# Three loads ahead of the second layer's turns: requested by sync instead of scalar, and scalar's table load two values earlier

## The reference, cut to what matters

```python
def _L1_xattn_ref(queries, keys, values, Wq, Wk, Wv, Wo):     # 16 heads of 16
    q, k, v = split_heads(queries @ Wq.T), split_heads(keys @ Wk.T), split_heads(values @ Wv.T)
    attn = softmax(einsum('bhqd,bhkd->bhqk', q, k) * scale)
    return einsum('bhqk,bhkd->bhqd', attn, v) (heads joined) @ Wo.T
x = x + _L1_xattn_ref(_layernorm(x), ctx, ctx, ...)
x = x + (_layernorm(x) @ W.T + b + _layernorm(x) @ V_r @ C.T)
```

## Time and profile before

| | us |
|---|---|
| median of 3 runs | 754.68 (752.0 to 754.7) |
| profiled execution, time | 749.47 |
| profiled execution, span | 747.7 |
| PE busy | 727.4 (97%) |
| DVE busy | 462.2 (62%) |
| ACT busy | 311.0 (42%) |
| POOL busy | 271.7 (36%) |

### The profile page before, as it was taken

How to read it: one execution, slowest core, us unless ns; L and a number is a source line. 1 busy time by engine, 2 the same in 40 slices (tenths; PEclk the granted TensorE clock), 3 DMA queues, 4 the chain that set the end, 5 groups by cost and what they waited for, 6 DMA issues and landing times.

```text
span 747.7 us, 15572 instructions
## 1 busy us (share of the span) xinstructions
PE 727.4 (97%) x5802; PEld 560.2 (75%) x5802; DVE 462.2 (62%) x1052; ACT 311.0 (42%) x556; POOL 271.7 (36%) x320
## 2 busy tenths in 40 slices
PE   8999999999999999999999999999998999999996
PEld 6776667666766575699999998989766667677774
DVE  4678663557355668534444655738677868788625
ACT  1323211422142121245555554644246755565571
POOL 5976225423410624402201515124734435205051
PEclk9999999999999999999999999999999999999998
DMA  9898944631521595722453423454887776755001
GB/s 263 224 301 265 203 117 154 187 122 41 180 71 52 188 374 171 250 59 82 118 143 88 126 76 95 121 143 133 244 223 193 183 184 175 199 140 127 28 3 50
DMA packets 73069, 113.87 MB, mean 152 GB/s; under 512 B 14930, under 2 KB 59347, under 8 KB 71075
## 3 DMA queue, kind: packets, MB, share of 16 engines
q1 hardware_dynamic: 60928, 80.17, 37.4%
q10 hardware_dynamic: 5906, 17.03, 8.4%
q0 software_dynamic: 6160, 15.67, 6.7%
HBM read 84.27 MB, written 28.41 MB: 151 GB/s over the span
## 4 chain that ended last, share of the span: by engine, by line
PE 87%; DVE 4%; POOL 2%; ACT 2%; issue 1%; DMA 1%; another core or an unknown queue 1%; ACTq 0%; SPq 0%; DVEq 0%; POOLq 0%
PE ps L1463 15%; PE ps L1092 12%; PE ps L1472 7%; PE ps L1109 7%; PE ps L2186 5%; PE ps L2215 5%; PE ps L1128 5%; PE ps L2206 4%; PE ps L1140 3%; PE ps L1062 3%; PE ps L1034 3%; PE ps L2179 2%; PE ps L2160 2%; DVE mxh L1836 2%; PE ps L1069 2%; PE ps L2115 2%
## 5 line engine op out<-in xcount | busy, mean ns | idle before, releaser
L1836 DVE TENSOR_REDUCE mxh<-ps 112x2 f32<-112x750 f32 x128 | 115.1, 932 | 34.2 <-PE ps L2186 31.3
L1463 PE MATMUL ps<-rowsT,w 128*128 128x128 f32 x1120 | 130.8, 275 | 0.0
L1463 PEld LDWEIGHTS ps<-rowsT,w 128*128 128x128 f32 x1120 | 128.0, 192 | 0.1
L2036 ACT ACTIVATE d_pT<-ps 125x448 f32<-125x448 f32 x192 | 92.0, 549 | 46.3 <-PE ps L2206 42.0
L1092 PE MATMUL ps<-x1T,sw 128*128 128x448 f32 x256 | 101.3, 540 | 0.0
L1417 ACT ACTIVATE w<-rw 128x1024 f32 x70 | 73.8, 1056 | 64.4 <-PE ps L1463 57.3
L1092 PEld LDWEIGHTS ps<-x1T,sw 128*128 128x128 f32 x256 | 47.6, 190 | 38.8 <-issue 35.9
L1356 POOL DMA_DIRECT2D yscr<-y x35 | 19.7, 563 | 153.8 <-DVE y L1390 153.8
L1472 PE MATMUL ps<-rw,h 128*128 x280 | 66.4, 380 | 0.0
L2186 PE MATMUL ps<-kst,qst 96*112 96x375 bf16 x256 | 58.4, 332 | 3.0 <-DVE mxh L1836 1.6
L902 ACT ACTIVATE silu<-ps,sb 128x448 f32<-128x448 f32 x32 | 20.3, 634 | 96.9 <-PE ps L1092 88.9
(11 more groups left out here) (259 smaller groups left out, 1193.3 us busy)
## 6 DMA issues: line engine op xcount, KB each, us to landing
kst<-kscr SPq DMA_DIRECT2D x39, 378.0 KB, 5.3
rw<-in_rw SPq DMA_DIRECT2D x24, 512.0 KB
kscr<-ka SPq DMA_DIRECT2D x16, 567.0 KB
cT<-in_ctx_t SPq DMA_DIRECT2D x17, 378.0 KB, 4.7
ctxT<-in_ctx_t SPq DMA_DIRECT2D x16, 378.0 KB
ctxn<-in_ctx SPq DMA_DIRECT2D x16, 336.0 KB
qst<-qscr ACTq DMA_DIRECT2D x12, 448.0 KB, 7.0
rows<-xg SPq DMA_DIRECT2D x35, 128.0 KB
```

What stands on the lines that cost most here:

```text
L1463: last = mm(bank[1 + 2 * q + k][:, block], w12[:, k, c, block], rowsT[:, q, c * P:(c + 1) * P], start=c == 0, stop=c == C - 1)
L1836: V.tensor_reduce(mxh[:, b % 2, 2 * g:2 * g + 2], ps[0:S, p:p + 2, 0:K], axis=AX_X, op=ALU.max).then_inc(s["s_max"], 1)
L2036: A(pT[:, q % 2, k, :], bank[4 + k][0:KC, 0:QUAD * S], ACT.Exp).then_inc(s["p_ready"], 1)
```

## The change

SP issues the keys of 2, the queries of group 1 and the keys of 3, each behind one of the three context loads of batches 13, 14 and 15; ACT no longer issues them. The one-element Exp, and with it the table load, moves from between values 14 and 15 to between values 13 and 14. No data, buffer, wait of TensorE or amount of work is changed.

```diff
@@ -1671,6 +1671,12 @@
         for b in range(NV, NV + 3):
             sp.wait_ge(s["v_ps"], b + 1)
             load_context(sp, b + 3)
+            if b == NV:
+                load_keys(sp, 2)
+            elif b == NV + 1:
+                load_queries(sp, 1)
+            else:
+                load_keys(sp, 3)
         maxima(0)
         load_values(1)
 
@@ -2045,17 +2051,14 @@
         for c in range(C):
             chunk_out(a, "q", EARLY - 1, c, bank[7 - 2 * c])
         late_values(NV)
-        load_keys(a, 2)
         for m in range(C):
             query_out(a, EARLY - 1, m, bank[7 - 2 * m])
         late_values(NV + 1)
         late_values(NV + 2)
-        load_queries(a, 1)
         late_values(NV + 3)
+
+        A(outT[0:1, 0, 0:1], mhalf[0:1, 0:1], ACT.Exp)
         late_values(NV + 4)
-        load_keys(a, 3)
-
-        A(outT[0:1, 0, 0:1], mhalf[0:1, 0:1], ACT.Exp)
         late_values(NV + 5)
         store_queries(a, EARLY - 1)
         for b in range(B - 1):
```

## The result

The median went from 752.95 us (16 runs, 751.09 to 754.7) to 756.26 us (16 runs, 753.46 to 759.38). The ratio is 1.0049 with a 95% interval of 1.0037 to 1.0061, which is +2.8 to +4.6 us. The profiled execution takes 755.69 us (span 753.9).

What follows compares the result with a forecast made beforehand. TensorE was taken to bound the kernel, with 87% of the chain. ScalarE 0, table load 0 and maxima rows behind the keys (context 15 included) +0.8 us, on 754.7, gave 755.5 us; range 751.5 to 758.3.

Steps and rivals of the forecast that it cites:

- ScalarE and the table load, 0: ScalarE's program: nine issues removed gain 0 to 0.1 us, taken as 0; table load ahead of values 14 costs 0.
- SP's issue times: SP: queries issued from 538.5, keys of 3 from 541.8, maxima from 543.7 instead of 542.42; that alone costs nothing.
- Step 1: Queue q1: queries, 1.36 MB at 0.242 MB/us, take 5.6 us, done at 546.6.
- step 2: Queue q1: context 15 takes 2.1 us, done at 548.7, needed at 548.50; TensorE late by 0.2 us.
- rival C: TensorE's wait ahead of values 15: context 15 late behind the queries; +3 us, both ends bad +4.5; chance 0.20.
- Steps 3 and 4: Queue q1: keys of 3 done at 553.45, then maxima rows at about 554.0; TensorE, wanting them at 552.09, held 1.9 us.
- The upper end of my price for the stand: First transposed scores: at 0.227 MB/us the maxima rows land at 555.3, TensorE held 3.2 us, cost 2.1 us.
- The deduction for VectorE, 1.1 us: First transposed scores: VectorE is the chain there, so a 1.9 us hold costs 0.8 us, one of 3.2 us costs 2.1.
- A: First transposed scores: maxima rows stand behind the keys of 3 in SP's queue; +0.3 to +2 us; chance 0.42.
- B: SP's queue: the order harms nobody, all lands by 552.3; ±0, 754.7; chance 0.30.
- D: ScalarE: its issues were in the way, so faster by 0.1 us or up to 1 us, 754; chance 0.05.
- I price no clock: TensorE from 552 to 554: busy 1.45 of 2 us, granted clock stays at 1.00, so no clock cost.

Runs made afterwards that it cites:

- the maxima ahead: Changed kernel with the queries of group 1 and keys of 3 requested by sync behind the maxima of batch 0 and values of 1; 1.0010 against before.
- one query copy ahead: Changed kernel with only the first of three query copies ahead of context 15, two behind it ahead of the keys of 3; 1.0050 against before.

## Why the prediction was right, and where its steps were wrong

The forecast was +0.8 us, to 755.5, with a range to 758.3; the change cost +3.7 us [+2.8, +4.6] and came to 756.26. That the time is so close is luck: the cost is more than four times the forecast one, and the kernel before has a median over 16 runs (752.95) that lies 1.7 us under the one over 3 runs that I started from, which makes up for part of it. The place and the kind of the cost were foreseen; the two delays in the queue were sized too small.

- **What bounds the kernel: right.** TensorE is the chain in the stretch. Filling 2.6 us of it in the kernel before costs 1.0037, +2.8 us.
- **ScalarE and the table load, 0: right.** Stretch cost 0.0 and 0.9998 for the table load alone. (One reading was off: other copies of values follow ScalarE idle times of 2.0 to 3.0 us too, not only 2.36 and 0.51.) Taking nine issues off ScalarE gains nothing: with the maxima ahead it is 1.0010.
- **SP's issue times: right** to 0.1 us, and the wait of SP for its own issues cost nothing.
- **Step 1, queries (done at 546.6), and step 2, context 15 (done at 548.7, 0.2 us late): wrong, and this is the first step that failed.** The working divided bytes by a mean rate. The mean was right: packets by queue, after, from 542 to 549.9 us,

```profile
q1 hardware_dynamic: 411, 1.82, 98.4%
```

  so 1.82 MB, more than queries and context together (1.75 MB), had passed by 549.9, which is 548.6 in before's time. But the context landed only at 552.64 (551.35 in before's time, 2.7 us later than forecast), and the last of the queries' 48 landings came at 550.83 (549.5, where 546.6 was forecast). A load has landed when its last part is through, and fifteen of the context's sixteen landings were in by 550.66. Others were by then carrying keys: from 550 to 552 the 13 packets of the context (those from 512 B to 2 KB) pass beside 39 of the keys (8 KB and more),

```profile
DMA packets 72, 0.49 MB, mean 246 GB/s; under 512 B 20, under 2 KB 33, under 8 KB 33
```

  I took the slowest engine only into rival C. Across the five runs with the three query copies ahead and the stand not filled, TensorE stood for 0.33, 1.46, 1.79, 2.08 and 2.57 us, and the sixteenth landing came 0.03, 1.7, 1.5, 2.2 and 2.0 us behind the fifteenth. The slack was misread as well: "over 3 us" before was 2.3 us (landed at 546.22, needed at 548.50).
- **Steps 3 and 4, the maxima at 554.0: wrong for the same reason.** In the changed kernel the keys of 3 landed at 556.83 and the maxima at 557.38, or 555.5 and 556.1 in before's time, where 553.45 and 554.0 were forecast; the 0.6 us between the two was right. With one query copy ahead and the same bytes in the queue they landed at 555.26, 1.2 us later than I had them; that stand was 3.47 us where 1.9 was forecast. With the queries on another queue, beside the keys, they landed at 558.44, or 557.1 in before's time, since the queries then start 2.9 us later. The upper end of my price for the stand was 3.2 us; in the four runs where it shows it was 3.47 to 5.5 us. In the changed kernel, and with the keys of 2 on scalar, the late context hides it. The deduction for VectorE, 1.1 us, was about right: the stand of 3.47 us cost 2.6 us in the stretch, with the clock low in part of it, and that of 1.00 us cost 0.1 us on top of its filling, 0.9 us less in both.
- **What the prediction didn't ask: when the maxima landed before.** It was at 551.77, only 0.3 us ahead of 552.09, though sync's queue held nothing large ahead of them but context 15. Their packets begin at 547.33, and from 544.0 to 550.7 the large packets of the queries on scalar's queue are under way. With the maxima ahead of both, and no query or key packet under way, they landed 1.4 us after their last issue; before it was 7.4 us. I read this as the other queue's share of the same engines; no run isolates it.
- **Rivals.** By the prediction's own sign, values of 15 past 549.5, it is C (chance 0.20) and not A (0.42): they started at 552.68, or 551.4 in before's time, the maxima landed at 556.1 where C has "556 or later", and +3.7 us is C's +3 and not A's +0.3 to +2. The experiments show that the delays of A and C are both in it, and they are not a sum. Putting one right leaves the other: queries behind the context, still 1.0050 to 1.0078; keys behind the maxima, 1.0016. Since TensorE waits first for the context and then for the maxima, the later of the two decides, and the keys of 3 ahead of the maxima are the larger part by the timed runs. B is refuted by every run with a stand. D is refuted by the table load alone and by the maxima ahead.
- **"I price no clock": wrong.** I looked at a stretch where TensorE was idle for parts of a microsecond and concluded for a stand of several. It cost 1.2 us more in the profiled execution.
- **The two rules.** The Trainium skill (DMA: Bandwidth & Descriptors, Issuing engines are not separate DMA queues) says that issuing from several engines only saves sequencer time, from which the prediction took that the change is worth nothing. The runs differ: the same nine copies by the same engine cost +0.8 us (interval -0.7 to +2.1) or +5.9 us depending on what they stand ahead of. By the Trainium skill (DMA: Bandwidth & Descriptors, Queues, rings and completion order) each DMA engine takes the descriptors of one queue in their order, and the runs agree: the context landed late wherever all three query copies stood ahead of it, and the maxima wherever the keys of 3 did.

Left open: why the last part of a load is so much behind the others, and by how much in an execution that isn't profiled; the 0.9 us that the changed kernel lost after the stretch; and the exact share of the clock in the timed difference. The spread of the changed kernel's runs (753.5 to 759.4) is wider than that of before in the same set (751.1 to 754.7), which would fit a tail that varies; but in another set before itself spread from 750.9 to 756.5, so this shows nothing.

## What to carry to other kernels

Here the loads that moved to another engine's queue cost nothing where they were issued and nothing where they landed; they cost what was queued behind them. So list what stands behind, and ask of each load when it is wanted and how long before that it lands now, the tiny ones too. Reckon a transfer to its last part, not to its mean rate: here the context came 2.7 us after the time that the mean rate gave. And a wait on TensorE that is long enough to let the clock fall is dearer than its length, so price both.

## What the runs showed of the hardware that I had not expected

- In the stretch the granted clock of TensorE fell to the 1.2 GHz level (0.50) around or after stands of 2.1, 2.6, 3.5 and 5.4 to 5.5 us. It stayed there for 3.4 us with the first three and for 6.8 us with the longest, 1.6 to 3.5 us of that while TensorE still stood. It stayed at 1.00 there with stands of 1.5 and 1.8 us, and with a stand filled by products whose results nobody reads. With 3.5 us it was still 1.00 while TensorE stood, and fell when it worked again (windows, one query copy ahead):

```profile
553.00:555.60 2.60, 0.00 (x0) 0.02 (x1) 1.01 (x4) 0.04 (x1) 0.00 (x0) 1.00 0.97 337
555.60:557.00 1.40, 1.39 (x16) 1.19 (x16) 0.41 (x1) 0.98 (x2) 0.00 (x0) 0.85 0.12 44
557.00:559.00 2.00, 2.00 (x15) 1.53 (x14) 1.49 (x3) 1.52 (x3) 0.00 (x0) 0.50 0.01 4
```

  The length of one stand doesn't decide it, though. In a later turn of four of the traces the clock fell after a stand of 1.5 to 1.7 us (with the maxima ahead of both: timeline of TensorE, then a window), and it stayed at 1.00 after one of 1.52 us in the changed kernel:

```profile
563.93 0.37 PE L2207 MATMUL ps<-qst,kst 128*128 128x112 bf16 x4 [1.66 <-ACT d_pT L2040]
```

```profile
566.00:568.00 2.00, 2.00 (x26) 1.38 (x19) 0.95 (x2) 0.61 (x2) 1.26 (x3) 0.50 0.87 260
```

- The last of three copies of 3.5 KB took 8 to 12 us to land behind 1 to 3 MB, with the DMA engines at a share of 0.97 to 0.99 in the four runs in which TensorE waited longest for it.
- A load of 378 KB landed 5.0 us after its issue behind one query copy of 448 KB, and 8.6, 8.8, 9.2, 9.5 and 10.0 us after it behind three (7.4 us with the queries alone moved): 1.2 to 2.5 us for each copy more, where such a copy takes 1.9 us at the rate of the earlier trace rows.
